# Scattering shorter rows: the expert computes its rows' weights itself

## The reference

```python
logits = x_flat @ gate_weight.T
scores = jax.nn.sigmoid(logits)
sfc = scores + e_bias[None, :]
# the four best groups of eight experts, then the eight best experts in them
topk_w = jnp.take_along_axis(scores, topk_idx, axis=1)
topk_w = topk_w / (topk_w.sum(-1, keepdims=True) + 1e-20)
return (topk_idx, topk_w * SCALE)
...
h = jax.nn.silu(jnp.einsum('ech,efh->ecf', xe, w1)) * jnp.einsum('ech,efh->ecf', xe, w3)
ye = jnp.einsum('ecf,ehf->ech', h, w2)
```

## Time and profile before

| | |
|---|---|
| median of 3 runs | 1486.03 us (1485.59 to 1489.81) |
| the profiled execution, its own time | 1486.32 us |
| its span | 1484.7 us |
| TensorE busy | 1160.4 us (78%) |
| VectorE busy | 693.5 us (47%) |
| ScalarE busy | 591.9 us (40%) |
| POOL busy | 328.3 us (22%) |
| DMA packets | 58030, 97.23 MB |

### The profile page before, as it was taken

The page is one execution under the profiler, slowest core; times in us unless marked ns, Lnnn a source line. Parts: engine busy times, 40 slices in busy tenths (PEclk is TensorE's granted clock), DMA queues, the critical chain, the costliest instruction groups (busy, mean ns, idle before and its releaser), DMA issues. The chain is left out here.

```text
span 1484.7 us, 15787 instructions
## 1 busy us (share of the span) xinstructions
PE 1160.4 (78%) x4501; PEld 643.7 (43%) x4501; DVE 693.5 (47%) x1944; ACT 591.9 (40%) x963; POOL 328.3 (22%) x325
## 2 busy tenths in 40 slices
PE   2565999999999999999998937539872738857772
PEld 1432444444444444444443425405541415445652
DVE  1115466445566445565446146538781724522221
ACT  1233455554455544455543202306741533014441
POOL 6600000000000000000000010070026054417664
PEclk9667999999999999999999957858985868969997
DMA  1020011120012110121110010267432010139997
GB/s 16 7 87 0 0 40 60 47 96 23 16 60 74 67 39 3 58 74 67 39 39 9 31 55 8 64 129 124 84 67 83 5 50 18 58 123 220 221 225 131
DMA packets 58030, 97.23 MB, mean 65 GB/s; under 512 B 11729, under 2 KB 39322, under 8 KB 57720
## 3 DMA queue, kind: packets, MB, share of 16 engines
q1 hardware_dynamic: 37800, 55.94, 14.4%
q0 software_dynamic: 20176, 40.65, 10.2%
HBM read 55.33 MB, written 53.00 MB: 73 GB/s over the span
## 5 line engine op out<-in xcount | busy, mean ns | idle before, releaser
L429 PE MATMUL b_ring<-b_H,b_w 128*128 128x512 f32 x512 | 224.8, 592 | 0.0
L429 PE MATMUL b_ring<-b_X1T,b_w 128*128 128x512 f32 x512 | 223.5, 595 | 0.0
L623 POOL TENSOR_TENSOR b_rstd<-b_veps,b_mhalf 128x4 f32<-128x4 f32 x32 | 32.6, 1018 | 707.2 <-DVE b_veps L69 707.2
L429 PE MATMUL b_ring<-XT,b_wqkv 128*128 128x512 f32 x384 | 174.7, 599 | 7.3 <-DMA b_wqkv<-in_wqkv 7.3
L429 PEld LDWEIGHTS b_ring<-b_X1T,b_w 128*128 128x128 f32 x512 | 96.4, 191 | 116.3 <-issue 109.6
L429 PEld LDWEIGHTS b_ring<-b_H,b_w 128*128 128x128 f32 x512 | 96.1, 190 | 115.3 <-issue 115.3
L1762 DVE TENSOR_REDUCE a_nmax<-a_pA 128x2 f32<-128x512 f32 x128 | 85.0, 688 | 80.7 <-PE a_pA L1473 44.5
L579 ACT ACTIVATE b_H<-b_ring,b_cur 128x512 f32<-128x512 f32 x128 | 88.0, 688 | 76.8 <-PE b_ring L429 69.7
L1734 ACT ACTIVATE a_ET<-a_pB 128x512 f32<-128x512 f32 x128 | 74.3, 595 | 88.1 <-PE a_pB L1495 56.8
L429 PEld LDWEIGHTS b_ring<-XT,b_wqkv 128*128 128x128 f32 x384 | 71.4, 193 | 86.1 <-issue 78.1
L680 DVE RECIPROCAL b_rec<-b_den 128x1024 f32<-128x1024 f32 x16 | 104.8, 6552 | 0.5
(11 more groups left out here) (287 smaller groups left out, 1778.1 us busy)
## 6 DMA issues: line engine op xcount, KB each, us to landing
xe<-b_nil POOLq DMA_DIRECT2D x16, 1284.0 KB, 5.3
x_wt<-in_wexp SPq DMA_DIRECT2D x32, 384.0 KB
x_rows<-xe SPq DMA_DIRECT2D x32, 321.0 KB
b_w<-in_w SPq DMA_DIRECT2D x8, 1024.0 KB, 5.3
b_wqkv<-in_wqkv SPq DMA_DIRECT2D x4, 768.0 KB
qparts<-q_part SPq DMA_DIRECT2D x24, 128.0 KB, 2.0
a_right<-qparts SPq DMA_DIRECT2D x16, 192.0 KB, 4.9
a_left<-qparts SPq DMA_DIRECT2D x16, 192.0 KB, 5.1
```

The lines of the kernel that those rows point to most:

```text
L429: last = pe.matmul(bank[:, :], lhsT(k), rhs(k), start=(k == 0), stop=(k == n_k - 1))
```

## The change

A scattered row has 272 numbers, 1088 bytes: the 256 of `x`, the token's number, the inverse of the token's sum of weights (times 2.5), and 14 zeros, which POOL writes once. VectorE no longer makes the 64 weights. The gate's row of each expert, as two columns of 128, is put behind its weights in the table `wexp`, so that a partition's part grows from 768 to 770 numbers. In the experts' phase TensorE multiplies the transposed rows with these two columns into `x_pW`, ScalarE takes the sigmoid (`x_score`), and VectorE multiplies it with the inverse from the row, which gives `x_share`. `s_hm` is now raised by this product instead of by the copy, and ScalarE waits for it before `x_ye`.

```diff
-XW = D + 1 + NEXP
+XW = D + 16
...
+            pool.memset(row[:, :, D + 2:], 0.0).then_inc(s_c, 1)
...
-                    link(dve.reciprocal(wrec[:, :], wsum2[:, :]))
-                    link(dve.tensor_tensor(wfull[:, :, :], w[:, :, :], wrec[:, :].unsqueeze(2).to_broadcast([P, TPC, NEXP]), ALU.mult))
+                    dve.reciprocal(row[:, l * TPC:(l + 1) * TPC, D + 1], wsum2[:, :])
...
-                    dve.tensor_tensor(row[:, l * TPC:(l + 1) * TPC, D + 1:XW], wfull[:, :, :], valid[:, :, :], ALU.mult)
...
-        WCOL = 2 * KD * HID + D
+        GCOL = 2 * KD * HID + D
+        WCOL = GCOL + KD
...
                     last.then_inc(s_u, 1)
+                    for i in range(SPE):
+                        for k in range(KD):
+                            last = pe.matmul(pW[e % 2][:, i:i + 1], rowsT[:, e % RINGX, k * CAP + i * P:k * CAP + (i + 1) * P],
+                                             wt[:, e % RINGX, GCOL + k:GCOL + k + 1], start=(k == 0), stop=(k == KD - 1))
+                    last.then_inc(s_sw, 1)
...
                     act.activation(sg[:, e % RINGX, :], pU[e % 2][:, 0, :], ACT.Sigmoid).then_inc(s_sg, 1)
+                    act.wait_ge(s_sw, i0 + e + 1)
+                    act.activation(score[:, e % RINGX, :], pW[e % 2][:, :], ACT.Sigmoid).then_inc(s_sc, 1)
                 if 2 <= s:
                     e = s - 2
+                    act.wait_ge(s_hm, i0 + e + 1)
...
-                e = dve.value_load(erow[0:1, 0, bass.ds(RINGX * l + s, 1)], min_val=0, max_val=NEXP - 1)
...
-                dve.tensor_copy(share[:, s % RINGX, :], rows[:, s % RINGX, :, bass.ds(e + D + 1, 1)].rearrange("p i o -> p (i o)")).then_inc(s_hm, 1)
...
+                    dve.wait_ge(s_sc, n)
+                    dve.tensor_tensor(share[:, e % RINGX, :], score[:, e % RINGX, :], rows[:, e % RINGX, :, D + 1], ALU.mult).then_inc(s_hm, 1)
...
-    experts = np.concatenate([w1, w3, i["L1_ffn_w2"].transpose(0, 2, 1)], 2)
+    gates = i["L1_ffn_gate_weight"].reshape(NEXP, KD, P).transpose(0, 2, 1)
+    experts = np.concatenate([w1, w3, i["L1_ffn_w2"].transpose(0, 2, 1), gates], 2)
```

More of the change, by code:

```diff
@@ L1225, in attention_router_phase @@
         wsum2 = sb("m_wsum2", [P, TPC])
-        wrec = sb("m_wrec", [P, TPC])
-        wfull, valid, slot, slot1 = gt, eq, eql, kept
+        valid, slot, slot1 = eq, eql, kept
         s8 = sb("m_s8", [P, TPC, TOPK])
@@ L1411, in _ @@
             pool.memset(lower[:, :, :], 1.0).then_inc(s_c, 1)
-            pool.wait_ge(s_c, 4)
+            pool.wait_ge(s_c, 5)
             pool.affine_select(out=before[:, :], in_=before[:, :], compare_op=ALU.is_gt, fill=0.0, base=0,
@@ L1563, in ranks @@
                 if l == 0:
-                    pe.wait_ge(s_c, 8)
+                    pe.wait_ge(s_c, 9)
                 pe.wait_ge(s_sc, l + 1)
@@ L1805, in constants @@
             def constants():
-                dve.wait_ge(s_c, 8)
+                dve.wait_ge(s_c, 9)
                 dve.tensor_copy(first[:, :], first_i[:, :]).then_inc(s_cc, 1)
@@ L2011, in experts_phase @@
         home = sb("x_home", [P, RINGX, SPE], I32)
+        score = sb("x_score", [P, RINGX, SPE])
         share = sb("x_share", [P, RINGX, SPE])
@@ L2022, in experts_phase @@
         pY = [pb(f"x_pY{i}", [P, SPE, D]) for i in range(2)]
+        pW = [pb(f"x_pW{i}", [P, SPE]) for i in range(2)]
         s_wt = [sem(f"x_weights{i}_loaded") for i in range(RINGX)]
@@ L2047, in experts_phase @@
         s_ye = sem("x_ye_ready")
+        s_sw = sem("x_scores_done")
+        s_sc = sem("x_scores_ready")
         block = ctx.enter_context(nc.Block())
@@ L2160, in body @@
                         last = pe.matmul(pY[e % 2][:, i, :], hid[:, e % RINGX, i * P:(i + 1) * P],
-                                         wt[:, e % RINGX, 2 * KD * HID:], start=True, stop=True)
+                                         wt[:, e % RINGX, 2 * KD * HID:GCOL], start=True, stop=True)
                     last.then_inc(s_y, 1)
```

## The result

The changed kernel took 1493.32 us in the median of 7 runs (1492.24 to 1497.08), beside 1488.88 us (1485.59 to 1491.02) for the kernel before in 7 runs: a ratio of 1.0035, 95% interval 1.0019 to 1.0051. It is slower by 4.4 us, where 1487 was forecast and 1492.5 was the upper end of the range. Of the 6.3 us between forecast and measurement, 2.85 are the base: the kernel before stood at 1486.03 us in the three runs that I forecast from, and at 1488.88 in seven. The rest is the change itself, +4.4 instead of the +1.2 of the sum. The profiled execution after took 1492.24 us, its span 1490.6 us.

A forecast was written before the change was run, and what follows sets the result against it. The DMA engines (97% busy) and a loop over two steps were taken to bind the experts together. Terms -1.65 + 1.5 - 0.1 + 1.2 + 0.2 = +1.2 us gave 1487 us, range 1480.5 to 1492.5.

The forecast's parts named there:

- The added products: Experts, TensorE: four one-column products per expert ahead of the down products, 4 x 0.113 = 0.45 us a step.
- rival (b): Experts: the loop over two steps binds, so the four products delay each load; 1490 to 1491.5 us, chance 0.17.
- Down products 3.7 instead of 3.25 us after the start of the transposes: Experts, sign expected in the profile after: down products end 3.7 us after the transposes start, instead of 3.25.
- 124 products of one column 0.11 us apart: Experts, sign expected in the profile after: 124 single-column products on TensorE, 0.11 us from one to the next.
- Start of the experts: First groups of experts, TensorE the bound at lower clock: products delay the load, +1.5 us, bounds 0.5 and 2.2.
- Steady steps: 24 expert steps held by DMA engines and two-step loop together: +0.05 us a step, +1.2 us in all.
- Tail: Last steps of the experts: 0 to 0.45 us added, 0.2 taken.
- Routing: VectorE's division and product dropped: -0.85 us in chunk 0, -0.4 each in chunks 1 and 2; together -1.65.
- Bytes in the experts: Experts' DMA: shorter row loads save about 0.12 us a step, less 3 ns for the longer weights.
- Lines: Experts' DMA: weights lose alignment, rows gain it; at most 4 ns a packet, 0.03 us a step, entered as 0.
- The scatters' standstill: Scatters into `xe`: VectorE and ScalarE stand still during POOL's back-to-back indirect DMAs, whatever their rows; change taken as 0.
- Rival (c): Scatter bursts: other engines' standstill depends on the rows' lines; -6 us, 1481, or down to 1449; chance 0.08.

The follow-up runs named there:

- routing alone: Changed kernel without the four products, sigmoid and VectorE's product, and with rows of 321 numbers as before; ratio 0.9999 to the kernel before.
- first experiment: Changed kernel without the four products, the sigmoid and VectorE's product, weights' table of 768 columns; 1419.26 against 1430.03 us for the kernel before, ratio 0.9933.

## Why the prediction failed, point by point

- **The added products: wrong, and the main cause of the loss.** This is the step that failed. I took 4 x 0.113 = 0.45 us a step from a row that counts passes, and read x16 as 16 products. It was 0.81 us: the down products start 3.03 us after the transposes (1405.77 to 1408.80) instead of 2.22. With 0.81 in place of 0.45 my rival (b), that the loop wins, would have had 1.5 x 0.81/0.45 = 2.7 us for the start and 0.81 - 0.12 = 0.69 us for two steps, 8.3 for 24: -1.65 + 2.7 - 0.1 + 8.3 + 0.2 = +9.5 us. The signs of (b) are what the profile shows: waits for rows fell from 29.7 to 9.8 us, POOL began to wait for results, the chain went through the products. But the loop doesn't bind alone: +9.5 is twice the measured +4.4, and the steps grew by 0.12 us in the first pair of profiles and by some 0.2 against the same kernel without products, not by 0.35 to 0.4. That the DMA engines and the loop both hold the step, as the forecast had it, stands; its price for the products was half of the true one. The earlier trace rows had shown the factor: the down products there, two in the code, stand as x4.
- **Down products 3.7 instead of 3.25 us after the start of the transposes:** they ended at 1409.91, 4.14 us after. **124 products of one column 0.11 us apart:** 248 records, 0.10 apart, so 0.20 from product to product.
- **Start of the experts, +1.5 (0.5 to 2.2):** up to the first reload +1.3 as forecast, by luck: with the true price it would have been 1.6 + 0.8 us, and the granted clock was higher this time (0.66 for 1318 to 1331 us; 0.52 in the same 13 us before), which is the likely reason that it wasn't; up to the ninth load +3.8, beyond the bound. I had stopped counting after three groups.
- **Steady steps, +0.05 (4.50):** measured 4.57, between the 4.50 and the 4.6 that I had named for (b). **Tail, +0.2 with 0.45 as the bound:** +1.85 in the profiles, above both; these last stretches scatter from 32.9 to 36.2 us over all the kernels (35.7 in the second profile of the kernel before), so its size is not settled.
- **Routing, -1.65:** chunk 0 right to 0.05 us. Chunks 1 and 2 were not the halves that I took. They gave up to 3 us or nothing, by the course that the phase took, and alone nothing in the total.
- **Bytes in the experts, -0.12 us a step:** not resolved. Without products the even part had 4.39 us a step with 272 numbers, 4.35 with 321 in the routing alone, and 4.45 and 4.47 with 321 in the kernel before: single profiles differ by as much as the effect. **Lines:** nothing to be seen beyond the intervals.
- **What I left out: bytes ahead of the experts.** The first experiment is 0.66% under routing alone, 9.4 us, of which my terms cover about 3. The first load came at 1259.6, 1259.75 and 1261.1 us in the three profiles with 321 numbers, and at 1254.6 in the mean of nine with 272 (1252.3 to 1258.3, the jobs near 1430). More than half of the gain thus lies ahead of the experts, where the same table is filled with empty rows (16 DMAs, each 1088 instead of 1284 KB, and one of a quarter of that) and rows are scattered. I had priced neither. In the means of these profiles the 5.5 us are 1.4 up to the phase ahead of attention's queries (the fill lies there), 1.3 in that phase (see the last section), 0.5 up to attention, and 2.3 from there on, where VectorE's shorter routing shows its 0.9 too. Neither fill nor scatter was tried alone.
- **The scatters' standstill, 0:** right for this change: 9.85 us of TensorE's work in 40, and 10.32 with rows of 258 numbers. Rival (c) is refuted: the rows became 15% shorter, and in the two bursts together TensorE did 14.88 us of work against 14.79 before. But my reason, that it goes with POOL's back-to-back indirect DMAs as such, has fallen too (last section).

The two errors had opposite signs, and that the forecast came near was luck. Against their own runs of the kernel before, the whole change came to +0.22% and the rows and routing to -0.67%, so the products with what hangs on them to +0.89%, 12.7 us (of which the products alone, put into the kernel before, made 0.55%); my terms for them were 1.5 for the start, 1.2 + 2.9 for the steps and 0.2 for the tail, 5.8. For rows and routing it was -9.6 us against my -4.65. Too little by 7 on one side and by 5 on the other left a forecast that looked close, +1.2 against +4.4, and that would have been further off with either error mended alone.

## What to carry to other kernels

Before a duration is multiplied, set the trace's count of an operation against the code's. Here a product of 32-bit numbers was two records (a transpose of them one), and a record took 0.10 us with one column and 0.11 with 64: such small ones cost their weight loads. Work added to this software pipeline cost most ahead of the instruction that releases the next load; behind it the same eight passes were nearly free, provided that what hangs on their result isn't put behind an unrelated wait. And when a table in memory changes its size, price every place that writes it, also where it is only filled. Last, a forecast that is a small difference of larger terms can come near the result with each of them wrong.

## What the runs showed that I had not expected

The kernel before took 1486 to 1489 us in the first measurements, 1496 in one job, and 1430 in the four others. The difference lies in the bursts of scatters. The same kernel, the same 0.97 us for each scatter, the same 40 us of the first burst:

```profile
1098.00:1138.00 40.00, 31.61 (x267) 19.65 (x269) 31.31 (x114) 23.98 (x47) 30.17 (x33) 0.86 0.28 99
```

TensorE has 31.61 us where the earlier trace rows shows 12.05, and VectorE 31.31 where it shows 5.60; from the start of attention to the first load it was 281 us instead of 334. So POOL's back-to-back indirect DMAs alone don't make the engines stand still; something outside of the kernel decides it. It isn't the chip, as far as its number tells: the jobs of 1430 us were on three chips, and the records give the job of 1496 the same number as one of them. What it is, these runs can't tell. It moves every kernel alike, as far as the ratios show, so that the comparisons within a job stand.

The clock's rise also shifts between kernels. In 12 us near the start of the phase before attention's queries, the granted clock was 0.50 with 321 numbers a row and 0.86 with 272, though nothing in those 12 us has to do with rows:

```profile
882.40:894.40 12.00, 11.95 (x36) 9.20 (x37) 1.96 (x10) 3.17 (x5) 0.00 (x0) 0.50 0.01 1
```
```profile
882.10:894.10 12.00, 11.22 (x54) 7.76 (x54) 4.49 (x17) 3.77 (x6) 0.00 (x0) 0.86 0.00 1
```

The first row is of the kernel before, profiled again, the second of the first experiment. That phase took 49.2 to 49.4 us with 321 numbers (four profiles), 47.9 to 48.2 with 272 (eleven), 50.6 with 273, 47.8 with 296, and with 258 once 47.8 and twice 49.4 to 49.5. It follows neither the length nor the line, but the clock: from the start of the phase it took 6 us to rise from 0.50 in the first experiment and 15 in the kernel before, and with 273 numbers it rose after 12 and fell back to 0.7. 1.3 us of the gain ahead of the experts stand there, and nothing in the diff points at them.
